# Edge sums over windows of 32 nodes in batches of two chunks, and the edge half of the first MLP layer inside the edge stage

## What is computed

```python
aggr = segment_sum(edge_attr_256, dst, 6250)             # 102.4 MB of edge rows are read once
h = relu(concat([layernorm(x), aggr], -1) @ W1 + b1)     # W1 is 512x256
h = relu(h @ W2 + b2)
x = x + h @ W3 + b3
y = layernorm(x)
w = softmax(((y @ W_x + b_x) @ W_slice + b_slice) / temp) # 8 heads x 64 slices, per node
tok = (w^T @ (y @ W_fx + b_fx)) / (sum(w) + 1e-5)
o = softmax(q k^T / 8) v                                 # 64x64 per head
out = x + (w @ o) @ W_out + b_out
```

## Time and profile before

| | us |
|---|---|
| median of 3 executions | 714.82 (714.66 to 717.14) |
| the profiled execution | 716.08 |
| its span, first to last instruction | 714.3 |
| TensorE busy with products | 689.7 (97%) |
| VectorE / ScalarE / GpSimd busy | 409.5 / 305.1 / 238.4 |
| moved by DMA | 131.72 MB |

### The profile page before, as it was taken

How to read it: one execution, slowest core, us unless ns; L and a number is a source line. 1 busy time by engine, 2 the same in 40 slices (tenths; PEclk the granted TensorE clock), 3 DMA queues, 4 the chain that set the end, 5 groups by cost and what they waited for, 6 DMA issues and landing times.

```text
span 714.3 us, 12349 instructions
## 1 busy us (share of the span) xinstructions
PE 689.7 (97%) x3510; PEld 431.3 (60%) x3510; DVE 409.5 (57%) x985; ACT 305.1 (43%) x470; POOL 238.4 (33%) x308
## 2 busy tenths in 40 slices
PE   7899999999999999999999989999999999799997
PEld 3666666666666666666556654444444444588886
DVE  6555545545555466453444378888888888522221
ACT  4233343333333434312221225545545545487773
POOL 3011011011010101313323336666666666254442
PEclk9999999999999999999999999999999999999999
DMA  8999999999999999200000004333333333212221
GB/s 314 393 375 408 393 406 408 407 405 404 407 404 404 394 384 313 75 1 0 0 0 0 0 1 60 73 70 62 73 71 62 72 73 66 38 59 73 81 81 65
DMA packets 95119, 131.72 MB, mean 184 GB/s; under 512 B 56825, under 2 KB 71117, under 8 KB 89983
## 3 DMA queue, kind: packets, MB, share of 16 engines
q1 hardware_dynamic: 94287, 131.26, 53.1%
q10 hardware_dynamic: 816, 0.26, 0.2%
HBM read 112.26 MB, written 6.40 MB: 166 GB/s over the span
## 4 chain that ended last, share of the span: by engine, by line
PE 75%; DMA 20%; DVE 2%; issue 1%; SPq 1%; ACT 0%; DVEq 0%; ACTq 0%
DMA ring_mem<-edge_attr_in 20%; PE ps L1124 14%; PE ps L1382 12%; PE ps L1293 12%; PE ps L1310 11%; PE ps L1246 6%; PE ps L1236 6%; PE ps L1228 6%; PE ps L1182 3%; PE ps L1286 2%; PE ps L1137 1%; PE ps L1174 1%; PE ps L1348 0%; DVE ring_mem L981 0%; DVE mx L983 0%
## 5 line engine op out<-in xcount | busy, mean ns | idle before, releaser
L1124 PE MATMUL ps<-ring_mem,side 128*64 128x256 f32 x1564 | 187.8, 386 | 8.1 <-DMA ring_mem<-edge_attr_in 6.0
L1124 PEld LDWEIGHTS ps<-ring_mem,side 128*64 128x64 f32 x1564 | 113.1, 137 | 68.8 <-issue 26.5
L756 DVE TENSOR_TENSOR side<-iota_w,rel 128x512 f32<-128x512 f32 x98 | 67.0, 686 | 94.2 <-PE ps L1137 94.1
L638 ACT ACTIVATE side<-ps 128x256 f32<-128x256 f32 (+1 forms) x98 | 40.7, 415 | 145.6 <-PE ps L1124 145.5
L1293 PE MATMUL ps<-ring_mem,xn 128*128 128x512 f32 x196 | 93.3, 599 | 0.9 <-DVE ring_mem L995 0.7
L1310 PE MATMUL ps<-side,ring_mem 128*128 128x512 f32 x196 | 92.3, 593 | 1.0 <-ACT ring_mem L674 1.0
L526 POOL TENSOR_TENSOR var_e<-mv,eps 128x2 f32<-128x2 f32 (+1 forms) x25 | 4.9, 195 | 237.8 <-DVE mv L822 237.8
L839 DVE TENSOR_TENSOR big<-big,ps 128x128 f32 x223 | 63.9, 287 | 30.1 <-issue 12.1
L1382 PE MATMUL ps<-side,ring_mem 128*128 128x256 f32 x360 | 77.9, 379 | 0.0
L584 POOL TENSOR_TENSOR ring_mem<-ring_mem 128x512 f32<-128x512 f32 x49 | 67.3, 1373 | 30.7 <-DVE ring_mem L995 30.1
L1382 PEld LDWEIGHTS ps<-side,ring_mem 128*128 128x128 f32 x360 | 68.4, 190 | 9.3
(11 more groups left out here) (131 smaller groups left out, 820.1 us busy)
## 6 DMA issues: line engine op xcount, KB each, us to landing
ring_mem<-edge_attr_in SPq DMA_DIRECT2D x97, 1024.0 KB, 8.6
x_sb<-x_in SPq DMA_DIRECT2D x24, 256.0 KB, 7.0
result<-ring_mem SPq DMA_DIRECT2D x24, 256.0 KB, 2.1
big<-side SPq DMA_TRANSPOSE x49, 3.0
ring_mem<-edge_attr_in SPq DMA_DIRECT2D x1, 512.0 KB, 5.9
ring_mem<-L_gnn_W_in SPq DMA_DIRECT2D x2, 256.0 KB, 3.3
ring_mem<-L_ffn_W_x_in SPq DMA_DIRECT2D x2, 256.0 KB, 4.7
ring_mem<-L_ffn_W_fx_in SPq DMA_DIRECT2D x1, 512.0 KB, 3.7
```

What stands on the lines that cost most here:

```text
L756: dve.tensor_tensor(hot[:, b], iota_w[:, :].unsqueeze(1).broadcast_to(shape), where.unsqueeze(2).broadcast_to(shape), ALU.is_equal).then_i ...
L1124: last = mm(ps[side_of * WINDOW:(side_of + 1) * WINDOW, SUM_BANKS[s % 2], pair * F:(pair + 1) * F], lhsT=hot[0:parts, s, t, :], rhs=ring8[ ...
```

## The change

- WINDOW is 32. Chunks up to 40 (TWOS) have 2 groups, all later ones 4. Four groups stand side by side in the array: two chunks of 2 groups share one PSUM column block, a chunk of 4 groups fills its own.
- The unit of work is a **batch** of two chunks, b = 0 to 49, two batches to a trip. TensorE runs the sums of both batches of a trip, 32 products, in a row; then for each batch of the trip its other work and its turn. A batch of 2-group chunks counts both its chunks as done at its end (`win_psum` + 2).
- SyncE reads 4 KB runs up to chunk 40 and 2 KB runs after it. From chunk 84 (FOURS) a chunk is 112 partitions high (896 edges), so that there are 100 chunks.
- The x half takes one pair of node tiles with each batch (instead of each trip) and ends in trip 13 of 25.
- From trip 14 on, each batch runs one half (m = 0 or 1) of `first_layer_edges`, the former `layer1`, for block i - 14 of the nodes: the windows are kept above a lowest node (`lowest`) that makes this block final by then. VectorE adds the result into `h1x` (`add_h1e`). Blocks 11 and 12 follow after the loop. `w1b_sb` and `w2_sb` are loaded ahead of trip 13.
- In the MLP stage TensorE runs only `layer2` and `layer3`; `layer2` alternates between two pairs of PSUM banks. ScalarE takes relu straight from `h1x`. The folds stand later.
- VectorE has a few more small operations at the start (`lowest`, and edges below a window marked as far).

```diff
-WINDOW = 64
+WINDOW = 32
...
+def run_batches(eng, step, ahead=None):
+    def trip(i, groups, parts, what):
+        for h in range(2 if ahead else 0):
+            ahead(i * 2 + h, h, i, groups, parts)
+        for h in range(2):
+            step(i * 2 + h, h, i, groups, parts, what)
+
+    trip(0, 2, P, "x")
+    trip(1, 2, P, "x")
+    with eng.Fori(2, TWOS // UNROLL) as i:
+        trip(i, 2, P, "x")
+    with eng.Fori(TWOS // UNROLL, X_TRIPS - 1) as i:
+        trip(i, 4, P, "x")
+    trip(X_TRIPS - 1, 4, P, "x")
+    trip(X_TRIPS, 4, P, "x")
+    with eng.Fori(H1E_TRIP, FOURS // UNROLL) as i:
+        trip(i, 4, P, "h1")
+    with eng.Fori(FOURS // UNROLL, H1E_TRIP + H1E_TILES - 1) as i:
+        trip(i, 4, LAST_P, "h1")
+    trip(H1E_TRIP + H1E_TILES - 1, 4, LAST_P, "h1")
...
# VectorE
+            def batch(b, h, i, groups, parts, what):
+                if isinstance(b, int) and b == 2:
+                    rest_of_table()
+                if before(b, BATCHES - 2):
+                    dve.wait_ge(win_psum, b * 2 + 2)
+                    for j in range(2):
+                        one_hot(b * 2 + (UNROLL + j), h * 2 + j)
+                if what == "h1":
+                    if h == 0:
+                        dve.wait_ge(h1x_ready, 2 * (X_PAIRS + 1))
+                    add_h1e(i - H1E_TRIP, h)
+                if h == 0:
+                    n_regs = UNROLL * groups
+                    dve.load(base_regs[0:n_regs], base_i[0:1, bass.ds(sums_ahead(b * 2, groups), n_regs)])
...
+                dve.wait_ge(sums_ready, b + 1)
+                turned_sums = ps[:, TURN_BANKS[h], :]
+                for j in range(2):
+                    c = b * 2 + j
+                    for g in range(groups if before(c, FULL_CHUNKS) else TAIL_GROUPS):
+                        dve.wait_ge(groups_added, sums_ahead(c, groups) + (CREDIT + g))
...
# TensorE
+            def one_sum(b, h, j, g, t, q, col, parts, first, last):
+                return mm(ps[q * WINDOW:(q + 1) * WINDOW, SUM_BANKS[h], col:col + F],
+                          lhsT=hot[0:parts, h * 2 + j, t, :], rhs=ring8[0:parts, h * 2 + j, t, :], start=first, stop=last)
+
+            def window_sums(b, h, i, groups, parts):
+                per = SUBTILES // groups
+                pe.wait_ge(hot_ready, b * 2 + 2)
+                pe.wait_ge(edge_in[h * 2], i * 16 + 16)
+                if groups == 2:
+                    pe.wait_ge(edge_in[h * 2 + 1], i * 16 + 16)
+                    for n in range(per):
+                        for q in range(4):
+                            last = one_sum(b, h, q // 2, q % 2, (q % 2) * per + n, q, 0, parts, n == 0, n == per - 1)
+                    last.then_inc(win_psum, 2)
+                    return
...
+            def batch(b, h, i, groups, parts, what):
...
+                if what == "x":
+                    if past(b, 3):
+                        first_layer_x(b - 3, 1 if isinstance(b, int) and b == X_PAIRS + 3 else 2)
+                    if past(b, 2) and before(b, X_PAIRS + 3):
+                        ln_transposes(b - 2, 1 if isinstance(b, int) and b == X_PAIRS + 2 else 2)
+                else:
+
+                    if h == 0:
+                        pe.wait_ge(w1b_in, 16)
+                        pe.wait_ge(h1x_ready, 2 * (X_PAIRS + 1))
+                        pe.wait_ge(groups_added, sums_ahead(b * 2, groups) + CREDIT)
+                    pe.wait_ge(h1e_added, (i - H1E_TRIP) * 2 + 1)
+                    first_layer_edges(i - H1E_TRIP, h).then_inc(h1e_psum, 1)
+                turn(b, h, groups)
```

More of the change, by code:

```diff
@@ L851, in chunk @@
+                if isinstance(b, int) and b == 2:
+                    far_flag()
+                if what == "x" and before(b, X_PAIRS):
+                    dve.wait_ge(x_in, b * 16 + 16)
+                    for a in range(2):
+                        norm_stats(b, a)
+                    if past(b, 1):
+                        dve.wait_ge(rstd1_ready, b)
+                    norm_sums(b, 2)
+                if isinstance(b, int) and b == X_PAIRS:
                     dve.wait_ge(x_tail_in, 16)
-                    norm_stats(EDGE_TRIPS, 0)
@@ L933, in fold_step @@
                 return folded[0]
+            for m in range(KF):
+                add_h1e(MLP_CHUNKS - 1, m)
+            for m in range(KF):
+                add_h1e(MLP_CHUNKS, m, n=1, bank=4)
             dve.wait_ge(fold_in, 16 * 5)
@@ new lines, in window_sums @@
+                pe.wait_ge(edge_in[h * 2], i * 16 + 16)
[6 more added lines that the diff above has]
+                    return
+                for j in range(2):
+                    tail = not before(b * 2 + j, FULL_CHUNKS)
+                    if j == 1:
+                        pe.wait_ge(edge_in[h * 2 + 1], i * 16 + (32 if tail else 16))
+                    for n in range(per):
+                        for g in range(TAIL_GROUPS if tail else groups):
+                            rows = TAIL_PARTS if tail and g == TAIL_WHOLE else parts
+                            last = one_sum(b, h, j, g, g * per + n, g, j * F, rows, n == 0, n == per - 1)
+                    last.then_inc(win_psum, 1)
@@ L1272, in _, with l2_banks, fold_transposes @@
-            last.then_inc(fold_t, 1)
-            layer3(1, 4)
-            with pe.Fori(2, MLP_CHUNKS - 1) as i:
-                layer2(i, 4 * P, l2_banks)
-                layer1(i + 1, 4 * P)
-                layer3(i, 4)
-            layer2(MLP_CHUNKS - 1, 4 * P, l2_banks)
-            layer1(MLP_CHUNKS, P)
+            def l2_banks(parity):
+                return [ps[:, 2 * parity + m, :] for m in range(KF)]
+            def fold_transposes():
+                pe.wait_ge(wx_in, 16 * KF)
+                pe.wait_ge(h1e_added, 2 * MLP_CHUNKS + 1)
+                for k in range(KF):
+                    for j in range(PAIRS):
+                        last = tr(ps[:, 6 + k, j * P:(j + 1) * P], wx[k][:, j * P:(j + 1) * P], ident[:, :])
+                last.then_inc(fold_t, 1)
@@ new lines, in _ @@
+            layer2(1, 4 * P, l2_banks(1))
+            pe.wait_ge(w3_in, 16)
+            pe.wait_ge(h1e_added, 2 * (MLP_CHUNKS + 1) + 1)
+            layer3(0, 4)
+            fold_transposes()
+            layer2(2, 4 * P, l2_banks(0))
+            layer3(1, 4)
+            fold_weights()
+            layer2(3, 4 * P, l2_banks(1))
+            layer3(2, 4)
+            fold_biases()
+            with pe.Fori(0, (MLP_CHUNKS - 4) // 2) as j:
+                for a in (0, 1):
+                    i = j * 2 + (4 + a)
+                    layer2(i, 4 * P, l2_banks(a))
+                    layer3(i - 1, 4)
@@ L1280, in _ @@
+            layer2(MLP_CHUNKS, P, [ps[:, 1, m * P:(m + 1) * P] for m in range(KF)])
             layer3(MLP_CHUNKS - 1, 4)
@@ L1321, in _ @@
             tp_rows(0, 0)
-            layer2(MLP_CHUNKS, P, [ps[:, 3, m * P:(m + 1) * P] for m in range(KF)])
             pe.wait_ge(fold_v, 7)
```

678 lines of the change are left out of this document (332 added, 346 removed).

## The result

The change made the kernel slower: 728.88 us median (720.13 to 730.27, 4 runs) against 715.98 (714.66 to 717.23, 4 runs), ratio 1.016 with a 95% interval of 1.010 to 1.022. The forecast was 689 us, 26 us faster, with a range that ended at 706. The profiled execution took 730.27 us, its span is 728.4.

A forecast was written before the change was run, and what follows sets the result against it. DMA and TensorE tie in the edge stage, TensorE bounds the MLP stage; that stage ends at 393.7 against 419.44 us, later work the same, so 714.82 - 25.7 = 689.1, forecast 689 us, range 680 to 706.

The forecast's parts named there:

- The bound before: Kernel before: edge stage a tie of DMA and TensorE at 11.0 us a trip; MLP stage bound by TensorE without gaps.
- the worth of the MLP stage: MLP stage: without layer1 in its blocks TensorE needs 91.8 us, ending at 393.7 against 419.44.
- The sums: Edge stage, TensorE's window sums: four strips overlap, 0.95 us a chunk, bounds 0.9 and 1.8.
- the rival of two strips: Edge stage sums: only two strips ever overlap, sums stay at 1.8 us a chunk, total 731 us; chance 0.13.
- Trips 0 to 13: Edge stage while node tiles are read (forecast: trips 0 to 12): DMA 11.7 us a trip bounds, TensorE needs 9.8.
- TensorE's slack of 1.9 us covers the new bunching of the ring: Trips with node tiles: slots freed two at once cost nothing, since TensorE has 1.9 us spare; DMA stays the bound.
- the rival of the cold array: Trips 14 to 24: waits drop TensorE's clock, their 8.3 us become 16.6, +60, total 750 us; chance 0.03.
- 2 KB runs: Edge transfers from chunk 40 on: 387 GB/s instead of 405, 380 with node tiles.
- the term of 5.3 us: Chunks 40 to 83: 46.1 MB at 387 instead of 405 GB/s costs 5.3 us.
- The loop's 10.8 us: Trips 14 to 24: edge half's ring of waits between TensorE and VectorE takes 10.8 us, bounds 9.5 and 12.0.
- The last four trips: Trips 21 to 24: 3.67 MB take DMA 9.5 us, so the 10.8 us loop bounds, 43.4 in all.
- Start of the ring: Start of edge stage: first sums wait for two chunks, adding 1 us, bounds 0 and 4.

The follow-up runs named there:

- e5: On top of e3, the edge half's two products a trip change places by half a trip; 692.86 us, ratio 0.971 to the kernel before.
- e2: Against the change: TensorE runs each batch's sums right ahead of that batch's other work; 709.77 us, ratio 0.992 to the kernel before.
- e3: Against the change: both edits, e1's loads 128 partitions high and e2's order of sums; 698.03 us, ratio 0.975 to the kernel before.
- m1: Transfers alone, no computing: edge-table pieces read ten at a time in twelve stages of different heights and run lengths; 386 GB/s at 128 partitions with 2 KB runs.
- e6: On top of e3, four dummy product instructions ahead of the edge half's first product in each trip from 14 on; 692.35 us, ratio 0.969.
- e1: Against the change: chunks of 112 partitions loaded 128 high with overlapping runs; 710.89 us, ratio 0.994 to the kernel before.
- e8: On top of e5, the first two batches sum chunk by chunk and free each slot at once; 691.75 us, ratio 0.967 to the kernel before.
- m3: Transfers alone, four slots: 112 partitions at different row starts, and 112 and 128 with and without TensorE products beside them; 112 carried 282 to 293 GB/s.

## Why the prediction was wrong, step by step

- **The bound before, and the worth of the MLP stage: right.** 92.6 us where 91.8 were forecast, and 294.6 us behind it against 294.9. That the transfers bound the edge stage fits e5, whose trips take 10.84 us at 387 GB/s.
- **The sums: right.** Two chunks take 1.93 us, and 1.07 for one of four groups, 0.95 a chunk forecast. Four strips work at once. One number beside them was wrong and cost nothing: by the prediction's own terms the rival of two strips decides from about 1.4 us a chunk on ((11.7 - 5.5 - 0.7) / 4 and (10.8 - 5.2) / 4), not from 1.65. By the strict order of the Trainium skill ("TensorE: Matmul & The Clock Gate", Part 3, "The mechanism") they would have taken 3.6 us; the 1.93 speak against that reading of it. The time came out near this rival's 731 by a wholly different way.
- **Trips 0 to 13: wrong, and the step is the sentence that "TensorE's slack of 1.9 us covers the new bunching of the ring".** I had compared two sums of busy time, 9.8 and 11.7 us, and called the smaller one covered. Slack counts only if it lies where the wait is. TensorE waited in the middle of the trip (3.94 us), and its work behind the wait, part of it at a clock of 0.62, ended late, so the slots of the first batch stood full and unread: 363 GB/s instead of e2's 389, about 10 us by the end of trip 14's sums, of the 13.0 that were missing there. Here too the rival of the cold array had a part, which no run separates.
- **2 KB runs: right.** 383 GB/s in e3 and in e5 from 130 to 190 us, 386 in m1 against 412 for 4 KB; the term of 5.3 us holds. That 4 KB runs cost nothing against 8 KB holds in the kernel (401 GB/s in e5 from 50 to 125 us, 402 before from 50 to 115), while alone they carried 412 against 424 (m1).
- **The loop's 10.8 us: right in its ring, short in its terms.** 11.04 measured (e6, and 11.03 and 11.04 in the change from 223.72 to 245.79). VectorE's idle time for the load of 16 registers was 1.25 us instead of 1.04. But the ring is one of waits, up to 2.6 us long, and the sentence that a fallen clock "also fills the gaps that made it fall" failed for a ring in which the slow product itself is a link. That took 5.7 us in e3. It is the rival of the cold array in kind, at a tenth of its price; as a whole that rival had been given a chance of 0.03.
- **The last four trips: wrong, the largest miss.** The step put 3.67 MB at 387 GB/s, 9.5 us, below the loop's 10.8. They took 15.8 each (63.0 us, where the forecast had 43.4; four times 10.8 is 43.2). Loaded 128 high they took 47.8 (e1). The rate of 128 partitions had been carried over to 112 although no row before showed another height; it should have stood among the unknown costs with a bound of its own.
- **Start of the ring: 1 us forecast, about 1.8 by the bytes of the first 50 us**, within the bounds of 0 and 4. It doesn't hang on the first slots: freeing them 3 us earlier (e8) moved nothing that can be measured.

With both wrong steps undone the kernel takes 698.0 us (e3), and 691.8 to 692.9 with the half-trip shift (e5, e8) or the warm products (e6) on top. That is near the forecast of 689, which was the time of a kernel whose ring runs full; but it is not this change's time, and e5 gets there by an order that the change doesn't have.

## A version that beats both

e5, e6 and e8 take 692.86, 692.35 and 691.75 us, ratios of 0.971, 0.969 and 0.967 to the kernel before, with intervals that overlap. Of the three I would keep e5: its trips are as short as the transfers (10.84 us), with no idle work in it. What bounds its edge stage is the rate of the transfers, from 50 us on.

## What to carry to other kernels

Compare no busy sums where buffers go round: draw the order landing, use, freeing for each slot over one trip, and ask what stands between a slot's landing and its use. When all uses of a trip are put in a row, the work that could cover the second landing is behind it. A long wait costs more than its length where the clock falls behind it. And when a tile's height changes, the transfer's rate is a new number to be measured; a taller transfer with rows that nobody reads can be the faster one.

## What the hardware showed beyond that

- Heights below 128 partitions, alone, in 2 KB runs (m1, one execution): 120 carried 212 GB/s, 112 280, 96 246, 64 203, against 386 for 128. It is not monotonic, a DMA share of 1.0 to 1.06 in all of them hides it, and two transfers of 64 and 48 (199) or 96 and 16 (217) are no way around.
- Runs of 8, 4 and 2 KB on 128 partitions: 424, 412 and 386 GB/s. The Trainium skill, "DMA: Bandwidth & Descriptors", Specifications, sees full rate from 512 B on; here 2 KB still cost 9%.
- Products of TensorE at full clock beside them changed the transfers by nothing (388 against 387 GB/s in m3). The Trainium skill, "SBUF — State Buffer", section "Who interferes with whom", says that engines and DMAs have separate ports; m3 agrees for TensorE, the one engine that it ran.
